# Sixteen routed experts on every token, or each expert on its own tokens alone

## The reference

```
h2     = layernorm(x2) * (1 + scale[b]) + shift[b]
scores = sigmoid(h2 @ gate_weight.T)                 # 16 experts in 4 groups
keep the 2 best groups, then the 4 best experts of a token
w      = scores of those 4, divided by their sum, times 2.5; 0 for the other 12
routed = sum over e of w[:, e] * (silu(h2 @ expert_up[e]) @ expert_down[e])   # 256 -> 128 -> 256
shared = silu(h2 @ shared_up) @ shared_down                                   # 256 -> 512 -> 256
out    = x2 + gate[b] * (shared + routed)
```

## Time and profile before

| | |
|---|---|
| median of 3 runs | 3187.55 us (3185.85 to 3205.73) |
| the profiled execution: its own time | 3187.41 us |
| its span, first to last instruction | 3185.6 us |
| mean granted TensorE clock | 0.817 of full speed |
| PE busy over the span | 2801.9 us, 88% |
| DVE, ACT, POOL busy | 1650.9, 1076.5, 618.1 us |
| chain that ended last, by engine | PE 35%, DVE 7%, POOL 6% of the span |

### The profile page before, as it was taken

One profiled execution on the slowest core, in us unless ns is written; L12 is line 12 of the kernel. 1 busy time (PEld: TensorE's weight loads), 2 busy tenths in 40 slices (PEclk: granted clock), 3 DMA queues, 4 the chain that ended last, 5 costly groups with the idle time before them and its releaser, 6 DMA issues.

```text
span 3185.6 us, 39962 instructions
## 1 busy us (share of the span) xinstructions
PE 2801.9 (88%) x13712; PEld 2052.0 (64%) x13712; DVE 1650.9 (52%) x4322; ACT 1076.5 (34%) x2142; POOL 618.1 (19%) x417
## 2 busy tenths in 40 slices
PE   4989994444998799999569999999999999999998
PEld 4966663333888678788446666666666666666665
DVE  3448883218142233333246665675656756667655
ACT  1258774233543111111123333323333233333231
POOL 1115552021100100000122122221222212222201
PEclk7579997665555666665679999999999999999999
DMA  3425557765663433434410011110111101111000
GB/s 97 139 93 164 162 172 194 184 131 129 148 140 103 136 108 109 129 87 129 159 40 19 29 47 47 48 47 1 47 47 48 47 1 47 47 47 47 7 1 14
DMA packets 348447, 269.81 MB, mean 85 GB/s; under 512 B 166284, under 2 KB 305996, under 8 KB 346724
## 3 DMA queue, kind: packets, MB, share of 16 engines
q1 hardware_dynamic: 337680, 256.90, 27.9%
q0 software_dynamic: 2304, 8.39, 1.0%
q10 hardware_dynamic: 8276, 2.10, 0.3%
HBM read 166.45 MB, written 100.89 MB: 84 GB/s over the span
## 4 chain that ended last, share of the span: by engine, by line
PE 35%; DVE 7%; POOL 6%; issue 2%; SPq 0%; DMA 0%; ACT 0%; POOLq 0%; DVEq 0%; ACTq 0%
PE mx_dn L1769 12%; PE mx_up L1755 11%; PE mx_m L1708 4%; POOL mx_st L1655 3%; DVE mx_acc L2060 3%; PE mx_m L1709 2%; PE mx_m L1717 2%; PE mx_m L1732 2%; POOL mx_rms L1666 1%; DVE mx_t L1922 1%; PE mx_m L1746 1%; POOL mx_acc L1673 1%; PE mx_m L1718 1%; POOL mx_acc L1676 1%; DVE mx_t L1943 1%
## 5 line engine op out<-in xcount | busy, mean ns | idle before, releaser
L2060 DVE SCALAR_TENSOR_TENSOR mx_acc<-mx_dn,mx_comb,mx_acc 128x256 f32<-128x256 f32 x1024 | 424.4, 477 | 476.5 <-PE mx_dn L1769 474.4
L1769 PE MATMUL mx_dn<-mx_edn,mx_hs 128*128 128x256 f32 x2048 | 513.3, 395 | 3.2 <-ACT mx_hs L1838 3.2
L1769 PEld LDWEIGHTS mx_dn<-mx_edn,mx_hs 128*128 128x128 f32 x2048 | 398.0, 197 | 168.2 <-issue 95.0
L1755 PE MATMUL mx_up<-mx_h2T,mx_eup 128*128 128x512 f32 x1024 | 496.2, 608 | 0.0
L1838 ACT ACTIVATE mx_hs<-mx_up 128x512 f32<-128x512 f32 x320 | 190.0, 596 | 789.8 <-PE mx_up L1755 789.5
L1755 PEld LDWEIGHTS mx_up<-mx_h2T,mx_eup 128*128 128x128 f32 x1024 | 189.2, 192 | 156.2 <-issue 147.0
L652 DVE SCALAR_TENSOR_TENSOR cv_acc<-cv_pre,conv_w,cv_acc 128x512 f32<-128x512 f32 x288 | 215.7, 750 | 88.8 <-ACT cv_acc L574 82.0
L516 PE MATMUL cv_pj<-cv_hT,wqkv 128*128 128x512 f32 x384 | 182.2, 605 | 13.4 <-ACT cv_acc L574 7.3
L1442 ACT ACTIVATE ds_U<-ds_ups 64x256 f32<-64x256 f32 x64 | 24.1, 377 | 419.0 <-PE ds_ups L1335 419.0
L1660 POOL TENSOR_TENSOR mx_t<-mx_vf,mx_ids 128x1024 f32<-128x1024 f32 x16 | 31.5, 1966 | 645.9 <-DVE mx_pr L1917 645.9
L1195 DVE TENSOR_TENSOR ci_prod<-ci_Ad,ci_T 128x62 f32<-128x62 f32 (+15 forms) x124 | 67.0, 540 | 148.9 <-DMA ci_Ad<-diag_d 144.6
(11 more groups left out here) (227 smaller groups left out, 4783.9 us busy)
## 6 DMA issues: line engine op xcount, KB each, us to landing
kqT_d<-cv_kqc SPq DMA_DIRECT2D x16, 1024.0 KB, 8.0
vf_d<-cv_vf SPq DMA_DIRECT2D x16, 1024.0 KB, 5.3
ds_kqT<-kqT_d SPq DMA_DIRECT2D x16, 1024.0 KB, 5.8
mx_vf<-vf_d SPq DMA_DIRECT2D x16, 1024.0 KB, 6.2
fl_toep<-taps_d SPq DMA_DIRECT2D x32, 392.0 KB, 5.1
fl_pool<-vf_d SPq DMA_DIRECT2D x8, 1216.0 KB
xin<-_attn_hidden_states_dram SPq DMA_DIRECT2D x16, 512.0 KB, 3.8
hT_d<-hT SPq DMA_DIRECT2D x16, 512.0 KB, 2.6
```

The lines of the kernel that those rows point to most:

```text
L1755: ins = pe.matmul(up_ps[x % 2][:], lhs, h2T[i][:, k, :], start=(k == 0), stop=(k == KD - 1))
L1769: ins = pe.matmul(dn_ps[(i + n) % 2][:, j, :], hs[x % 4][:, j * P:(j + 1) * P], rhs, start=(x == 0 and j % 2 == 0) or x >= NS, stop=(x >= ...
L2060: ins = dve.scalar_tensor_tensor(out=acc[i][:, j, :], in0=dn_ps[(i + n) % 2][:, j, :], scalar=comb[i][:, j, e:e + 1], in1=acc[i][:, j, :], ...
```

## The change

Each expert works on its own tokens alone, 4 of 16 per token.

- **Places.** When a unit is routed, `count` on PE (5 short matmuls) and `rank` on DVE (9 operations of up to 256 elements a partition) work out the row that each of the token's 4 choices gets in its expert's region of a DRAM buffer `X_d`. POOL writes each normalised row there 4 times: `scatter`, 16 indirect DMAs of 128 rows of 1 KB for a unit.
- **Tables.** After a batch row's fourth unit, `tables` on DVE (13 operations, some of 1280 elements on one partition, then 3 for each unit) lists 80 tiles of 128 rows, each with its first row and its expert; 64 tiles would hold the 8192 chosen rows, the rest is room for ends that aren't full. `pads` on SP writes 16 blocks of zeros behind the regions.
- **Tiles.** One batch row later, 20 tiles run in each body. For a tile SP reads two registers from the tables and issues two loads, the rows and the expert's up weights (`xload`, 128 KB each, 4 buffers). PE reads a register, transposes twice (`turn`), multiplies up on 128 columns (`raise_`) and down on 256 columns (`lower`), for three successive tiles in a slot; ACT modulates and takes Silu; ACT and DVE in turns copy the result, SP stores it (`ystore`).
- **Sums.** Two batch rows later POOL gathers the 4 result rows of each token (`gather`, 16 indirect DMAs for a unit) and DVE sums them (`total`, 4 times 6 operations on 128x256). x2 and the shared expert's result go to DRAM in between and come back.
- **Order.** A body has 24 slots (4 shared, 20 tiles) over which the 40 steps are spread. There are 24 bodies: 4 with shared and mix alone, 12 with tiles too, of which the last 8 gather as well, 4 with tiles and gathers (batch row b = 4), 4 with gathers alone (b = 5). Loops are unrolled.
- **Buffers.** The five loads, x2 and h2T have one buffer in place of two. `load(u + 2)` waits for x2 of unit u+1 and stands in SP's queue behind slot 21.

The core of the diff, all of it in `mix_and_experts` but for the first lines:

```diff
+CAP = L + P
+ROWS = (E + 1) * CAP
...
-        vf = [sb(f"mx_vf{i}", [P, J, 2 * D]) for i in two]
...
+        vf = sb("mx_vf", [P, J, 2 * D])
...
+            def load(u):
+                rows = slice(u * J, (u + 1) * J)
+                i = u % 2
+                if u:
+                    sp.wait_ge(x2_done, 2 * u)
+                sp.dma_start(vf[:], m.vf_d[rows].rearrange("j p c -> p j c")).then_inc(loaded[i], 16)
+                sp.dma_start(fl[:], m.fl_d[rows].rearrange("j p c -> p j c")).then_inc(loaded[i], 16)
+                sp.dma_start(dl[:], m.o_d[rows].rearrange("j p c -> p j c")).then_inc(loaded[i], 16)
+                sp.dma_start(xx[:], x_v[u]).then_inc(loaded[i], 16)
+                sp.dma_start(hT[:], m.hT_d[u]).then_inc(loaded[i], 16)
+            def pads(b):
+                sp.wait_ge(tab_done, b + 1)
...
+                for e in range(E):
+                    r = sp.value_load(tab_p[b % 2][0:1, e:e + 1], min_val=0, max_val=2 * ROWS - P)
+                    sp.dma_start(m.X_d[bass.ds(r, P), :], zrow[:]).then_inc(pad_out, 16)
...
+            def xload(n):
+                b, t = n // NTL, n % NTL
+                r = sp.value_load(tab_s[b % 2][0:1, t:t + 1], min_val=0, max_val=2 * ROWS - P)
+                e = sp.value_load(tab_e[b % 2][0:1, t:t + 1], min_val=0, max_val=E - 1)
+                if n >= 4:
+                    sp.wait_ge(tup_done, n - 3)
+                sp.dma_start(xt[n % 4][:], m.X_d[bass.ds(r, P), :]).then_inc(xt_in[n % 4], 16)
+                sp.dma_start(eup[n % 4][:], w.expert_up[bass.ds(e, 1)].squeeze(0).rearrange("(k p) i -> p k i", p=P))\
+                    .then_inc(xt_in[n % 4], 16)
...
+            def ystore(n):
+                b, t = n // NTL, n % NTL
+                if t == 0 and b >= 2:
+                    sp.wait_ge(sum_done, TB * (b - 1))
+                sp.wait_ge(yt_done[n % 2], n // 2 + 1)
+                sp.dma_start(m.Y_d[b % 2][t * P:(t + 1) * P, :], yt[n % 4][:]).then_inc(yt_out[b % 2][n % 4], 16)
+            def cload(v, j):
+                n = v * J + j
+                if n >= 2:
+                    sp.wait_ge(out_st[n % 2], 16 * (n // 2))
+                sp.wait_ge(acc_out, 16 * (v + 1))
+                sp.wait_ge(x2_out, 16 * (v + 1))
+                sp.dma_start(co[n % 2][:], m.sh_d[v, :, j, :]).then_inc(c_in[n % 2], 16)
+                sp.dma_start(cx[n % 2][:], m.x2_d[v, :, j, :]).then_inc(c_in[n % 2], 16)
+            def put(v, j):
+                n = v * J + j
+                sp.wait_ge(sum_done, n + 1)
+                sp.dma_start(out_v[n], co[n % 2][:]).then_inc(out_st[n % 2], 16)
...
+            for b, g, u in bodies():
+                v = u - 2 * UB
+                for x in range(NX):
+                    n = u * PER - NTL + x - NS
+                    if 1 <= b <= B:
+                        if g == 0 and x == NS - 1:
+                            batch_ready(b - 1)
+                            xload(n + 1)
+                            xload(n + 2)
+                        if x >= NS:
+                            if (n + 2) % NTL >= 2:
+                                xload(n + 2)
+                            if n >= 3:
+                                ystore(n - 3)
+                    if b >= 2:
+                        if x in (4, 5, 13, 17):
+                            cload(v, (4, 5, 13, 17).index(x))
+                        if x in (10, 14, 18, 22):
+                            put(v, (x - 10) // 4)
+                    if b < B and g == UB - 1 and x == 16:
+                        pads(b)
+                    if x == 21 and u + 2 < NU:
+                        load(u + 2)
...
+            def scatter(u, j):
+                b = u // UB
+                pool.wait_ge(place_done, u + 1)
+                if u % UB == 0 and j == 0 and b >= 1:
+                    pool.wait_ge(xT_done, NTL * (b - 1) + 1)
+                for k in range(TOPK):
+                    n = column(u, j, k)
+                    pool.indirect_dma_start(m.X_d[:, :], bass.IndirectOffsetOnAxis(ap=idx[b % 2][:, n:n + 1], axis=0),
+                                            xn[u % 2][:, j * D:(j + 1) * D], None).then_inc(scat[u % 2], 16)
+            def gather(v, j):
+                b, n = v // UB, v * J + j
+                if v % UB == 0 and j == 0:
+                    pool.wait_ge(idy_done, b + 1)
+                    for r in range(4):
+                        pool.wait_ge(yt_out[b % 2][r], 16 * NTL // 4 * (b // 2 + 1))
+                if n >= 2:
+                    pool.wait_ge(sum_done, n - 1)
+                for k in range(TOPK):
+                    c = column(v, j, k)
+                    pool.indirect_dma_start(G[n % 2][:, k, :], None, m.Y_d[b % 2][:, :],
+                                            bass.IndirectOffsetOnAxis(ap=idy[b % 3][:, c:c + 1], axis=0))\
+                        .then_inc(G_in[n % 2], 16)
+            deviations(0)
+            products(0)
+            rms_root(0)
+            ln_root(0)
+            for b, g, u in bodies():
+                v = u - 2 * UB
+                more_mix = u + 1 < NU
+                if more_mix:
+                    deviations(u + 1)
+                if b >= 2:
+                    gather(v, 0)
+                    gather(v, 1)
+                if more_mix:
+                    products(u + 1)
+                if b >= 2:
+                    gather(v, 2)
+                if b < B:
+                    scatter(u, 0)
+                    scatter(u, 1)
+                if more_mix:
+                    rms_root(u + 1)
+                if b >= 2:
+                    gather(v, 3)
+                if b < B:
+                    scatter(u, 2)
+                    scatter(u, 3)
+                if more_mix:
+                    ln_root(u + 1)
...
+            def turn(n):
+                b, t = n // NTL, n % NTL
+                if t == 0:
+                    pe.wait_ge(tab_done, b + 1)
+                expert[n] = pe.value_load(tab_e[b % 2][0:1, t:t + 1], min_val=0, max_val=E - 1)
+                pe.wait_ge(xt_in[n % 4], 32 * (n // 4 + 1))
+                if n >= 2:
+                    pe.wait_ge(hTt_done, n - 1)
...
+                for k in range(KD):
+                    ins = pe.transpose(xT_ps[n % 2][:, k * P:(k + 1) * P], xt[n % 4][:, k * P:(k + 1) * P], m.ident[:])
+                ins.then_inc(xT_done, 1)
+            def raise_(n):
+                pe.wait_ge(hTt_done, n + 1)
+                if n >= 2:
+                    pe.wait_ge(tsilu_done, n - 1)
...
+                for k in range(KD):
+                    ins = pe.matmul(up_ps[n % 2][:, 0:P], eup[n % 4][:, k, :], hTt[n % 2][:, k, :],
+                                    start=(k == 0), stop=(k == KD - 1))
+                ins.then_inc(tup_done, 1)
+            def lower(n):
+                pe.wait_ge(tsilu_done, n + 1)
+                if n >= 2:
+                    pe.wait_ge(yt_done[n % 2], n // 2)
+                pe.matmul(dn_ps[n % 2][:, 0:D], hst[n % 2][:], edn[:, bass.ds(expert[n], 1), :].squeeze(1),
+                          start=True, stop=True).then_inc(tdn_done, 1)
...
+            for b, g, u in bodies():
+                nxt = u + 1 if u + 1 < NU else None
+                turned = max(0, (u - UB) * PER)
+                if b < B:
+                    up(u, 0, turned - 1)
                 for x in range(NX):
+                    n = u * PER - NTL + x - NS
+                    ss = list(steps(x)) if nxt else []
+                    if b < B and x < NS:
+                        if x < NS - 1:
+                            up(u, x + 1, turned - 1)
+                        for s in ss[:1]:
+                            mix(nxt, s)
+                        down(u, x, turned)
+                        ss = ss[1:]
+                    if 1 <= b <= B and x >= NS:
+                        turn(n)
+                        if n >= 1:
+                            raise_(n - 1)
+                        if n >= 2:
+                            lower(n - 2)
+                    for s in ss:
+                        mix(nxt, s)
+                    if b < B and x == 10:
+                        count(u)
...
+            def modulate(n):
+                b = n // NTL
+                act.wait_ge(xT_done, n + 1)
+                if n >= 2:
+                    act.wait_ge(tup_done, n - 1)
+                for k in range(KD):
+                    ins = act.activation(hTt[n % 2][:, k, :], xT_ps[n % 2][:, k * P:(k + 1) * P], ACT.Identity,
+                                         scale=m.mod[:, 8 + k, b:b + 1], bias=m.mod[:, 6 + k, b:b + 1])
+                ins.then_inc(hTt_done, 1)
+            def tile_silu(n):
+                act.wait_ge(tup_done, n + 1)
+                if n >= 2:
+                    act.wait_ge(tdn_done, n - 1)
+                act.activation(hst[n % 2][:], up_ps[n % 2][:, 0:P], ACT.Silu).then_inc(tsilu_done, 1)
...
+            def rank(u):
...
+                dve.wait_ge(count_done, u + 1)
```

(44 more changed lines are left out.)

564 lines of the change are left out of this document (362 added, 202 removed).

## The result

Slower by more than forecast: 3761.6 us (median of 4 runs, 3752.5 to 3762.4) against 3196.6 beside it, a ratio of 1.175 (95% interval 1.168 to 1.182). The forecast was 3390 with 3720 as its upper end. The profiled execution spans 3750.8 us. From the first shared matmul to the end it has about 2110 us where the sum had 1747, so 363 us are to be explained.

What follows compares the result with a forecast made beforehand. PE's work bound the old kernel; one unit's closed chain would bound the new. Bodies 1364, tables 30, late loads 30, clock 48, last bodies 180 + 95 sum to 1747 us, 203 more: 3390 us, 6% slower, range 3160 to 3720.

Steps and rivals of the forecast that it cites:

- p: POOL's price for issuing one indirect DMA, put between 0.75 and 2.9 us and taken as 1.2 us.
- `load(u + 2)` stands behind slot 21 on SP: 2.5 us late: Next unit's loads in SP's queue: 2.5 us late in 12 bodies, 30 us in the sum.
- The closed round: Chain from one x2 through loads, statistics, logits, mix and projection to the next x2: 77 us with only shared work beside it.
- From slot 10 to 17 the tiles are free: PE runs through these tiles in 16 us, then waits for the mix, some 26 us after the logits.
- A tile's own pace of 2 us: Two load issues and a landing, 4.3 us over 2.3 slots, give 1.9 us; register reads were taken as 0.3.
- Rival E: Register reads cost over 1 us each, tiles 3.5 us, PE 112 us: 380 us more, 3770 us; chance 0.08.
- Half of the tables' 14 us: Tables on DVE take 14 us, half hidden while POOL scatters: 7.5 us for each of 4 batch rows.
- the 7 us taken off for the full clock: Statistics to x2: some 14 us of PE work at the low clock gets shorter, so 57 us instead of 63.7.
- the clock term: PE idles some 15 us in every unit and starts again low: 3 us a unit, 48 in the sum.
- Rival C: Indirect DMAs on POOL are dear, delayed by DVE on a shared port pair: p = 2, 3650 us; chance 0.12.
- B: Rival: not slower, bodies of 70, 77 and 79 us, 3075 us; steady body under 81; chance 0.25 with partial versions.
- D: Rival: clock stays at 1.2 GHz beside the tiles, PE's 66 us become about 130: 3890 us; chance 0.05.

Runs made afterwards that it cites:

- e8: Changed kernel with all tile result copies on ACT and the tile stores issued by ACT instead of SP: 3573.8 us.
- e11: The changed kernel unaltered, run again as a control; its profile shows no remote waits: 3686.6 us.
- e16: Changed kernel with SP loading tile tokens and up weights from fixed places, so without register reads on SP: 3614.3 us.
- e13: The changed kernel unaltered, control of a later group; its profile shows 157 us of remote waits: 3756.0 us.
- e15: Changed kernel with plain DMAs of the same size for the indirect scatters; gathers stay indirect: 3623.2 us.
- e3: Changed kernel with a unit's five loads issued as their buffers come free, only x after its x2: 3682.4 us.
- e1: Changed kernel with every tile's result copied by ACT, none by DVE: 3714.7 us.
- e9: Changed kernel with six edits: ACT copies, early unit loads, roots before scatters, eight tile buffers, tables moved, pads moved: 3523.1 us.
- e6: Changed kernel with eight buffers for tile tokens and up weights instead of four, loads six tiles ahead instead of two: 3665.2 us.
- e12: Changed kernel with 80 unread matmuls on PE ahead of the projection in the four bodies without tiles: 3721.5 us.
- e14: Changed kernel with 40 unread matmuls on PE ahead of the projection in the four bodies without tiles: 3747.4 us.
- e4: Changed kernel with plain DMAs of the same bytes for all indirect ones, scatters and gathers: 3576.4 us.

## Why the prediction was wrong in size

**What held.** Direction, and the claim that the preparation's chain, not PE's work, would set the unit. DVE's first statistics do wait for the load of hT (9 us in each body) and the root of the mix for its own scatters (8.97 us). p was taken as 1.2 us; the pace of a row is 1.27. The end took 100.5 us for 95. Tables on DVE took 14.2 us, as reckoned.

**The term that failed most: "`load(u + 2)` stands behind slot 21 on SP: 2.5 us late".** The 11 bodies with tiles miss by 20.5 us each. The closed round can be read in two parts: from x2 (L2244) to the next unit's first statistics (L2166), and from there to that unit's x2. A round without tiles, then one with them:

```profile
1718.84 0.69 DVE L2244 TENSOR_TENSOR mx_x<-mx_x,mx_m 128x512 f32<-128x512 f32 x1 [1.54 <-issue]
1719.60 0.37 SPq L1689 DMA_DIRECT2D mx_vf<-vf_d  x1
1733.48 0.60 DVE L2166 BATCH_NORM_STATS2 mx_bs<-mx_vf 128x6 f32<-128x64 f32 x4 [9.36 <-DMA mx_hT<-hT_d]
```

```profile
2192.87 0.69 DVE L2244 TENSOR_TENSOR mx_x<-mx_x,mx_m 128x512 f32<-128x512 f32 x1 [3.62 <-remote]
2203.17 0.46 SPq L1724 DMA_DIRECT2D Y_d<-mx_yt  x1
2203.68 0.43 SPq L1689 DMA_DIRECT2D mx_vf<-vf_d  x1
2215.76 0.61 DVE L2166 BATCH_NORM_STATS2 mx_bs<-mx_vf 128x6 f32<-128x64 f32 x4 [9.07 <-DMA mx_hT<-hT_d]
```

Without tiles SP issues the load of the next unit at once. With them it stands behind the loads and stores of the tiles, and goes out 10.0 to 14.5 us after x2, and 24.1 and 26.1 with the pads in front. Eleven rounds, from x2 at 1985.7 to x2 at 3252.3, take 1266.6 us (the first still starts without tiles). Of these 286 lie between x2 and the statistics, where the sum had 12 + 2.5 us each, 160: 127 of the 225 us. Relieving SP shows the cause: this part is 234 us in e8 against 281 in e11, and 246 in e16 against 284 in e13. That is 47 and 38 us of what these two won in the bodies (61 and 57). Plain scatters leave it at 280 (e15). It can't be won back whole by issuing the loads earlier: e3 took them out of the round and gained some 5 us a body.

**"From slot 10 to 17 the tiles are free".** The other part, from the statistics to x2, takes 71.4 us without tiles and 86 to 88 in most rounds with them, where the sum had 68 and 77 to 80, the clock's 3 among them. I let PE run through the tiles and then wait at the transposes of the mix. It never waited there. The tiles were not independent of the chain: L2431 on DVE, L1724 and L1715 on SP close them to it, and every engine works in order. The prediction asks who is queued behind a late step and answers "the next load, scatter and sum"; it left out the tile's own copy and, through it, store and loads. Taking the copy off DVE gave 46 us of the bodies (e1 against its base), a fifth of the 225. e8 with its 61 against e11 adds SP's relief to that, and the 150 of e9 contain other edits too. What lengthened this second part most were the indirect scatters: plain ones shorten it from 982 to 885 us (e13, e15), with the stalls and DVE's wait for the root.

**"A tile's own pace of 2 us".** 100 tiles took 363 us, 3.6 each with the first tile's wait for its tables and pads. I divided issue and landing by the slots they may take, as for a latency. SP's queue is a server: a store, two reads and two issues one after the other, 2.75 us, and a pair of loads for each sum. e6 excludes latency, e16 the DMA rate. The reads cost 0.65 us each on SP, for which I had put 0.3. Rival E had the total nearly right (3770) by luck. It made the reads cost over 1 us each, and PE the bound at 112 us a unit, but PE is busy 80 of 109; only that the reads are dear in the tile's pace was right.

**Pads.** 20.4 us of SP for each batch row, ahead of tile loads, are in no term. The change's code has them. Half of the tables' 14 us was put beside POOL's scatters; in bodies with tiles they cost 24 and 24 us over the body before, pads included.

**Bodies without tiles: 85.3 against 80.** The parts are 13.9 us from x2 to the landed load (12 reckoned), rank 2.6 (3.5), a delay of the root by 8.97 - 2.97 = 6.0 (4.5), and the rest 62.8, where the first unit had 63.7 alone. So the 7 us taken off for the full clock came to 0.9, and only 3 of them were put back by the clock term. The chain alone leaves PE idle for 24.4 and 5.4 us, and PE runs at the lower level behind both (6.11 us for the projection, 3.62 in the steady unit). e12 shows that idle time brings the lower level. That the level is what kept the 6 us is not shown: e12 lengthened the body by its own matmuls, and e14 didn't keep the clock.

**The stalls beside indirect DMAs.** No term had them. They are worth 2094 - 2024.5 = 70 us of S, about 19 of them behind the last copy. Rival C, which made indirect DMAs dear by POOL waiting for DVE, had the sign but not the way: POOL's own pace stayed at 1.27, and it was the others that stood still. Plain scatters are worth 144 us, at most half of that stalls by the difference of the bases, since some stayed.

**Rivals B and D.** No body with tiles of the unaltered kernel came under 95 us (the point for B was 81). PE was never full (51 to 87 us busy a body), at a clock of 0.68 to 0.80, so D's 130 us of PE work did not bind.

By place, the miss of 363 us is 24 in bodies without tiles, 127 between x2 and the statistics, 91 from there to x2, 8 at the edges of the rounds, 108 in the last 100 tiles and 5 in the gathers. By cause it is less clean. The stalls are 70, and the two tables-and-pads bodies about 33 beyond their term, much of it the late load again. SP's serial queue and the coupling through DVE are shown as causes (e16: 156 us of S, e8: 105), but they overlap, and no run splits them.

## What to carry to other kernels

Work that is cheap on the engine that was the bound is not free if its helpers stand in the queues of the long chain: for each small step of it (copy, store, load) name the queue, and what that queue waits for just then. Then look at what stands behind it in that queue: here the load of the next unit, which closes the round, was issued 10 us late behind three tiles. Cost a queue that issues DMAs as a server, all reads, issues and stores of one item added up, before asking about bytes or landing. And when a change replaces dense work by a chain, first see what the chain takes alone; here the closed round of 78 to 85 us was within 20% of the old unit's 97.5 before a single tile was added.

## What the runs showed of the hardware

- An indirect DMA of 128 rows of 1 KB from POOL: 0.96 us with a gap of 0.30, and 1.77 or 1.98 for the first behind a tensor operation. The same plain: 0.54.
- While rows of such scatters are issued, DVE, ACT and SP can stand still until the last is out, up to 8 us, in some groups of executions and in none of others with the same kernel; 70 us of 3760. Rows of indirect gathers do it too (e15), plain DMAs don't (e4). SP's issues were held as well: a load went out at 2285.55, as the row of scatters ended at 2285.56, 4.17 us behind the end of the store ahead of it, where two register reads take 1.30. DMA: Bandwidth & Descriptors (SWDGE vs HWDGE vs iDMA) in the Trainium skill says that DMAs issued from SP or ACT are immune to one interference, that of DVE's locks with the descriptors of POOL's DMAs. What is seen here is another, and no run shows that one.
- The same page (Issuing engines are not separate DMA queues) says that issuing from several engines saves only sequencer time, usually small. Here that time was the pace of the tiles: moving stores of 128 KB from SP to ACT took 45 us off 100 tiles, dropping two register reads 99.
